# The last batch of three cross attentions: squares copied by three engines, inverses spread earlier, the product written straight into the output array

## The reference

```
scores  = einsum('bhsr,bhlr->bhsl', q_r, k_r)     # 56 queries of 16 heads against 1500 keys
attn    = softmax(scores, axis=-1)
ctx_c   = einsum('bhsl,bld->bhsd', attn, kv_r)    # 64 features per query and head
x       = x + (ctx_c folded with w_kc_kv and Wo)  # the projection that follows
```

## Time and profile before

| what | value |
|---|---|
| median of 3 runs | 3149.91 us (3147.82 to 3156.69) |
| profiled execution, its own time | 3146.17 us |
| its span | 3144.3 us |
| mean granted TensorE clock | 0.959 |
| DVE, ACT, POOL busy | 1877.9, 1242.5, 1230.3 us |
| `scatter`, GpSimd, 128x448 (line 1613) | 15 per layer, 1.8 us each |
| copies of squares, GpSimd, 32x768 (line 1602) | 128 per layer, 0.82 us each |
| the three turns end (start of line 557, PE) | 638.9, 1707.6, 2649.2 us |

### The profile page before, as it was taken

How to read it: one execution, slowest core, us unless ns; L and a number is a source line. 1 busy time by engine, 2 the same in 40 slices (tenths; PEclk the granted TensorE clock), 3 DMA queues, 4 the chain that set the end, 5 groups by cost and what they waited for, 6 DMA issues and landing times. The chain is left out here.

```text
span 3144.3 us, 48214 instructions
## 1 busy us (share of the span) xinstructions
PE 2904.8 (92%) x17993; PEld 1699.2 (54%) x17997; DVE 1877.9 (60%) x3657; ACT 1242.5 (40%) x1997; POOL 1230.3 (39%) x1127
## 2 busy tenths in 40 slices
PE   4899999969999889899999989989899999587999
PEld 3655655545455463355556567653355556345444
DVE  5548888842222257798895143347788885654222
ACT  3446666611111142466663122222466663523221
POOL 4228888700334024466664000004466664211000
PEclk8889999989999989999999999999999999888999
DMA  1136566514122112255563010012255553001111
GB/s 33 45 102 150 142 149 143 126 30 132 40 102 87 65 40 76 55 133 137 134 145 102 11 48 21 26 44 80 55 137 135 146 129 79 16 12 24 41 40 34
DMA packets 203011, 255.17 MB, mean 81 GB/s; under 512 B 121034, under 2 KB 142908, under 8 KB 200332
## 3 DMA queue, kind: packets, MB, share of 16 engines
q1 hardware_dynamic: 202204, 250.91, 30.7%
q10 hardware_dynamic: 576, 1.18, 0.1%
HBM read 120.52 MB, written 21.38 MB: 45 GB/s over the span
## 5 line engine op out<-in xcount | busy, mean ns | idle before, releaser
L1802 ACT ACTIVATE l2x_shared<-l2x_shared,l2x_a_low 128x1500 f32<-128x1500 f32 x112 | 173.3, 1547 | 149.8 <-DVE l2x_shared L1754 149.8
L1802 ACT ACTIVATE l1x_shared<-l1x_shared,l1x_a_low 128x1500 f32<-128x1500 f32 x112 | 173.3, 1547 | 149.5 <-DVE l1x_shared L1754 149.5
L1802 ACT ACTIVATE l0x_shared<-l0x_shared,l0x_a_low 128x1500 f32<-128x1500 f32 x112 | 173.3, 1547 | 138.5 <-DVE l0x_shared L1754 137.2
L1353 POOL TENSOR_TENSOR l2x_q_straight<-l2x_q_straight,l2x_q_crossed 128x448 f32<-128x448 f32 x48 | 54.6, 1137 | 340.3 <-DVE l2x_q_crossed L1344 340.3
L2046 DVE TENSOR_TENSOR l0f_times_up<-l0f_gate,l0f_U 128x448 f32<-128x448 f32 x64 | 39.8, 621 | 237.0 <-PE l0f_U L1964 237.0
L1666 PE MATMUL l2x_a_S_ps<-l2x_kt,l2x_a_q 64*128 64x366 f32 (+1 forms) x896 | 173.3, 502 | 1.0 <-DVE l2x_shared L1754 0.7
L1666 PE MATMUL l1x_a_S_ps<-l1x_kt,l1x_a_q 64*128 64x366 f32 (+1 forms) x896 | 173.4, 503 | 0.6 <-DVE l1x_shared L1754 0.6
L1666 PE MATMUL l0x_a_S_ps<-l0x_kt,l0x_a_q 64*128 64x366 f32 (+1 forms) x896 | 172.5, 502 | 0.6 <-DVE l0x_shared L1754 0.5
L1602 POOL COPY l1x_space<-normed 32x1024 f32<-32x1024 f32 x128 | 132.6, 1036 | 90.6 <-DVE normed L1770 83.6
L1602 POOL COPY l2x_space<-normed 32x1024 f32<-32x1024 f32 x128 | 132.6, 1036 | 88.5 <-DVE normed L1770 81.6
L2015 ACT ACTIVATE l0f_gate<-l0f_G 128x448 f32<-128x448 f32 x72 | 39.2, 544 | 310.8 <-PE l0f_G L1959 310.8
(11 more groups left out here) (678 smaller groups left out, 6718.1 us busy)
## 6 DMA issues: line engine op xcount, KB each, us to landing
l0x_space<-normed SPq DMA_DIRECT2D x128, 128.0 KB
l1x_space<-normed SPq DMA_DIRECT2D x128, 128.0 KB, 2.3
l2x_space<-normed SPq DMA_DIRECT2D x128, 128.0 KB, 2.3
l0x_space<-l0x_a_blocks SPq DMA_DIRECT2D x124, 96.0 KB, 3.6
l1x_space<-l1x_a_blocks SPq DMA_DIRECT2D x124, 96.0 KB, 3.2
l2x_space<-l2x_a_blocks SPq DMA_DIRECT2D x124, 96.0 KB, 3.0
l0f_gu<-in_L_ffn_gu SPq DMA_DIRECT2D x36, 256.0 KB, 2.6
l0x_a_q<-l0x_qa SPq DMA_DIRECT2D x32, 224.0 KB
```

What stands on the lines that cost most here:

```text
L1353: pool.tensor_tensor(straight[:, n % 2, k], straight[:, n % 2, k], crossed[:, k], ALU.add).then_inc(rotated, 1)
L1802: act.activation(p[:, n % 2], p[:, n % 2], ACT.Exp, bias=low[:, n % 2, 1:2], scale=-1.0, accum_out=den[:, b % 2, k:k + 1]).then_inc(exp_re ...
```

## The change

Only the last batch's end changes, in each of the three layers. The eight copies of group 1 of batch 15 are divided: GpSimd copies two, ScalarE two (behind its four DMA issues), VectorE four (behind its last `block_turn` and the inverse). GpSimd does its two before `scatter(14)`, which now comes last on it. TensorE spreads all seven columns of inverses in one go, after slots 4 to 6 of group 0, into a bank of `T_ps`; ScalarE copies them to `rrow`. The sums stay in `C_ps`: VectorE multiplies them by `rrow` and writes `ct` in its own order. The last `keep_contexts` of ScalarE and the last copy of GpSimd are gone.

```diff
+    LAST_POOL, LAST_ACT = [(2, 2), (3, 3)], [(0, 0), (1, 1)]
+    LAST_DVE = [(l, (l + 1) % 4) for l in range(4)]
...
+                def own_last():
+                    pool.wait_ge(inner_blocked, N)
+                    pool.wait_ge(outer_blocked, N)
+                    pool.wait_ge(valued, 2 * (B - 1))
+                    pool.wait_ge(kept_own, OWN * (2 * B - 1))
+                    for k, (l, qi) in enumerate(LAST_POOL):
+                        if k > 0:
+                            pool.wait_ge(last_pool, k)
+                        pool.tensor_copy(*part_at(1, l, qi)).then_inc(last_pool, 1)
+                    pool.wait_ge(last_pool, len(LAST_POOL))
...
+                    if b + 1 == B:
+                        own_last()
                     if b > 0:
                         scatter(b - 1)
-                    own(b, 1)
-                scatter(B - 1)
+                    if b + 1 < B:
+                        own(b, 1)
...
-                            pe.wait_ge(kept_own, OWN * (2 * b + g + 1))
+                            if b + 1 < B or g == 0:
+                                pe.wait_ge(kept_own, OWN * (2 * b + g + 1))
+                            else:
+                                pe.wait_ge(last_pool, len(LAST_POOL))
+                                pe.wait_ge(last_act, len(LAST_ACT))
+                                pe.wait_ge(last_dve, len(LAST_DVE))
...
+                def spread_inverses():
+                    pe.wait_ge(rden_ready, B)
+                    pe.wait_ge(pt_kept, N)
+                    for k in range(T):
+                        for odd in range(2):
+                            last = pe.matmul(T_ps[odd * CW:(odd + 1) * CW, N % 2, k * 64:(k + 1) * 64],
+                                             rden[:, (B - 1) % 2, k:k + 1].to_broadcast([128, CW]),
+                                             m.ident[:, odd * CW:(odd + 1) * CW], start=True, stop=True)
+                    last.then_inc(spread, 1)
...
                 for k in range(T, T + 6):
                     for piece in PIECES[k]:
                         values(B - 1, *piece)
+                    if k == T:
+                        spread_inverses()
...
+                def own_last():
+                    dve.wait_ge(inner_blocked, N)
+                    dve.wait_ge(outer_blocked, N)
+                    dve.wait_ge(valued, 2 * (B - 1))
+                    for l, qi in LAST_DVE:
+                        dve.tensor_copy(*part_at(1, l, qi)).then_inc(last_dve, 1)
...
-                    dve.wait_ge(c_kept, 2 * b + g + 1)
-                    dve.tensor_tensor(cn[:, b % 2, a:z], cn[:, b % 2, a:z], C_ps[:, g, 256:256 + z - a], ALU.mult).then_inc(normed, 1)
+                    dve.wait_ge(valued, 2 * b + g + 1)
+                    dve.wait_ge(spread_kept, 1)
+                    dve.tensor_tensor(ct[:, :, b, a // 8:z // 8], C_ps[:, g, 0:z - a].rearrange("c (s h) -> c h s", h=8),
+                                      rrow[:, b % 2, a:z].rearrange("c (s h) -> c h s", h=8), ALU.mult).then_inc(normed, 1)
...
                 move(act, B - 1, 1, range(2, 4))
-                keep_contexts(B - 1, 0)
-                keep_contexts(B - 1, 1)
+                for l, qi in LAST_ACT:
+                    act.copy(*part_at(1, l, qi)).then_inc(last_act, 1)
+                act.wait_ge(spread, 1)
+                act.wait_ge(scattered, B - 2)
+                act.copy(rrow[:, (B - 1) % 2], T_ps[:, N % 2, 0:C // 2]).then_inc(spread_kept, 1)
```

More of the change, by code:

```diff
@@ L1483, in attend @@
         r_loaded = [st.sem(f"{name}r_loaded{j}") for j in range(2)]
+        last_pool = st.sem(name + "last_pool")
+        last_act = st.sem(name + "last_act")
+        last_dve = st.sem(name + "last_dve")
+        spread = st.sem(name + "spread")
+        spread_kept = st.sem(name + "spread_kept")
         normed = st.sem(name + "normed")
@@ L1603, in own @@
                             done += 1
-                def scatter(b):
[L1606 to L1610, removed]
+                def own_last():
[8 more added lines that the diff above has]
+                    pool.wait_ge(last_pool, len(LAST_POOL))
+                def scatter(b):
+                    pool.wait_ge(kept_own, OWN * (2 * b + 3))
                     pool.wait_ge(c_kept, 2 * b + 2)
@@ L1705, in values @@
                             last.then_inc(pt_used, 1)
[L1706 to L1716, removed]
+                    if end == NS:
+                        last.then_inc(valued, 1)
+                def spread_inverses():
[7 more added lines that the diff above has]
+                    last.then_inc(spread, 1)
                 if ctx is not None:
```

## The result

The changed kernel takes 3133.43 us (median of 8 runs, 3120.62 to 3146.29) against 3150.0 us before (8 runs, 3147.31 to 3156.69). The ratio is 0.9938, interval 0.9922 to 0.9953: 15 to 25 us faster; the medians lie 16.6 us apart.

What follows compares the result with a forecast made beforehand. PE, busy 92% of the span, was taken as the bound, losing time only when idle or at lower clock. Ends' 17.7 us plus 1.56 of clock make 19.3; 3148.9 less that is 3129.5, own range 3125 to 3134.

Steps and rivals of the forecast that it cites:

- Case B: Ends of turns: PE waits for transfers' signals, not GpSimd; only the tail shrinks, 5 us gained, 3144 us; chance 0.06.
- Where PE will be: Group 1's first pieces, each layer: PE is through 0.4 us later for the longer spread, at 628.1, 1699.6 and 2639.0.
- the lower bound: Spread ahead of group 1: twelve more instructions cost 0.35 us by first starts or 0.48 by busy time; 0.4 taken.
- Will the squares be there?: Last batch's eight copies: each engine's share ends before PE arrives, so PE doesn't wait and the copies cost nothing.
- the lower bound of 0.624: VectorE's copy of 768 columns: 0.624 us at least, the time for 448 columns; 1.07 each at most.
- The products: Group 1's 32 last products: with no idle time ahead, 2.82 us in all three layers.
- The tail: Behind the products: three steps become one multiply of 0.45 us plus 0.1 for the semaphore.
- the upper bound of 0.54: VectorE's new multiply of 192 columns: at most 0.54 us with a step of eight elements, at least 0.35.
- The sum: Ends of the three turns: gains of 7.1, 4.2 and 6.4 us, together 17.7; 19.3 with layer 2's projection.
- The clock of the projection: Layer 2's projection: a shorter PE gap ahead of it saves 1.56 us lost to the lower clock.
- The time: Whole kernel: 3148.9 us, the two lowest timed runs' average, less 19.3 gives 3129.5; chance 0.79.

Runs made afterwards that it cites:

- order alone: Against the kernel before, GpSimd copies all eight squares of the last batch ahead of the scatter of batch 14, nothing else changes; 3138.36 us, ratio 0.9956.
- the repeat: The changed kernel, unaltered, measured once more; 3130.82 us (9 runs) against 3149.07, ratio 0.9933.
- the kernel before once more: The kernel before the change, unaltered, profiled again; one run, 3147.32 us.
- tail alone: Against the changed kernel, GpSimd copies all eight squares behind the scatter of batch 14; the new spread and multiply stay; 3142.7 us, ratio 0.9972.

## Why the prediction was right, point by point

- **PE waits for GpSimd, not for transfers.** Right: with the squares earlier, every wait of line 1701 fell, with order alone from 4.29 to 0.94. Case B is out.
- **Where PE will be.** Arrival at 6.9 us after the reciprocal was forecast (628.1 - 621.20), 6.68 was measured (635.70 - 629.02). Twelve more instructions of the spread cost 0.82 - 0.47 = 0.35, the lower bound, and the rows of group 1's two pieces (lines 1721 and 1723) overlap by 0.17 us, which I had not taken off.
- **Will the squares be there?** They were, though the sizes were off. GpSimd's copies took 0.82 to 1.15 us instead of 0.876, ScalarE's 0.832 each (0.79 forecast). VectorE's four took 4.8 us in layers 0 and 1, inside 2.5 to 4.3 only for layer 2 (3.34). The mis-sized term is VectorE's: a copy alone is 0.55, under the lower bound of 0.624, but behind a GpSimd instruction it waits that out. In layer 0 the last one ended at 634.33; PE needed it at 635.70, so of 2.5 us in hand 1.4 were left. The Trainium skill's SBUF — State Buffer (Who interferes with whom) says that a copy can take the pair of ports that VectorE shares with GpSimd, and that the one that issues later is then blocked for the other's whole instruction. The trace agrees: the copy that started 0.36 us behind the 2.01 us scatter took 2.07 us and ended 0.42 us behind it. My working had left this out. Had the scatter taken 1.4 us longer, PE would have waited, by this reading. The tightest share was ScalarE's in layer 1: it ended at 1698.67, 0.9 us ahead of PE, where 0.4 to 0.9 were forecast.
- **The products.** 2.77 us in all three layers (2.82 forecast), at a granted clock of 1.00, the 2.4 GHz level.
- **The tail.** The multiply of 192 columns took 0.49 (0.35 in order before), between the 0.45 that I took and the upper bound of 0.54. From the products' end to the projection's start it is 639.33 - 638.47 = 0.86 us (0.85 forecast).
- **The sum.** Forecast 7.1 + 4.2 + 6.4 = 17.7 for the ends, measured 7.4 + 4.5 + 6.2 = 18.2, the repeat 18.6. Layer 2 lost 0.5 us to a transfer of group 0 that came late (0.27 us of wait in the fence above, and the 0.17 by which the rows overlap where nothing is waited for) and had none in the repeat. The clock of the projection brought 1.65 us against 1.56. The size and the reason, the shorter gap, were right; that the loss before stood in layer 2 was luck of the one profile that I had, and in the kernel before once more it stands in layer 0.
- **The time.** 19.3 us forecast, 19.8 in the trace, 15 to 25 timed; the medians lie 16.6 us apart, and 18.3 in the repeat. The 3.9 us between forecast and median are in the spread of the runs: 3120.6 to 3146.3 for the changed kernel, 3140.1 to 3170.8 in a later set of 32 for the one before, and 14.6 us between the earliest and the latest start of layer 0's last reciprocal (614.4 and 629.0) over ten profiles. I had read 3147.8 to 3156.7 as the kernel's whole scatter.

## What to carry to other kernels

Before dividing late work among engines, look at what stands ahead of it on its own engine: putting the last copies before work that nobody waits for gave 11.2 of 18.2 us, the division among three engines 1.9. Price a wait of TensorE with its clock: gaps of about 3 us cost up to 1.7 us more in the products behind them, and gaps of 2.2 to 2.5 us ahead of the projection cost as much in 4 of 12 cases. Compare ends of stages, not spans of two profiles, when another stage scatters by more than the effect.

## What the runs showed of the hardware

- The same copy of 32x768 floats on VectorE took 0.55 us alone and 2.07 us beside a 2.0 us multiply on GpSimd; GpSimd's copy went from 0.82 to as much as 1.15 us beside VectorE's.
- A gap of TensorE does not decide its clock by its length alone: after 2.95 us the granted clock stayed at 1.00 (before, layer 1), after 2.82 us (tail alone, layer 1) it was 0.50 and the products took 4.50 instead of 2.82 us. After 2.2 us ahead of the projection it was 1.00 in one layer and 0.50 in another of the same run (before, once more).
- ScalarE's four issues of the same transfers took 2.76 us in layer 0 and 3.92 in layer 1 of the changed kernel (2.77 and 4.27 before), SyncE's four beside them 3.93; in layer 1 of the kernel with all squares on ScalarE they took 2.46. What holds them up is open.
